# Last expert layer of a two-layer graph block: gated expert rows added into DRAM, instead of gathered and summed in SBUF

## The reference, cut to what matters

```python
def _L1_ffn_ref(x, Wg, bg, W1, b1, W2, b2):          # 8 experts, hidden width 384
    xf = x.reshape(-1, d)                            # x is the layer norm of the tokens
    logits = xf @ Wg.T + bg
    probs = softmax(logits)
    top2_vals, top2_idx = top_k(probs, 2)
    cw = zeros((n, 8)).at[arange(n)[:, None], top2_idx].set(top2_vals)
    h = gelu(einsum('nd,edh->neh', xf, W1) + b1[None])
    y = einsum('neh,ehd->ned', h, W2) + b2[None]
    return einsum('ne,ned->nd', cw, y)
...
x = x + _L1_ffn_ref(_layernorm(x)[None], ...)[0]
```

## Time and profile before

| | |
|---|---|
| Median of three runs | 2000.32 us |
| The profiled execution, its own time | 1999.16 us |
| Its span, first to last instruction | 1997.3 us |
| TensorE (PE) busy | 1838.2 us, 92% |
| VectorE (DVE) busy | 745.1 us, 37% |
| ScalarE (ACT) busy | 401.4 us, 20% |
| GpSimd (POOL) busy | 128.5 us, 6% |
| Mean granted TensorE clock | 0.964 |

### The profile page before, as it was taken

One profiled execution on the slowest core, in us unless ns is written; L12 is line 12 of the kernel. 1 busy time (PEld: TensorE's weight loads), 2 busy tenths in 40 slices (PEclk: granted clock), 3 DMA queues, 4 the chain that ended last, 5 costly groups with the idle time before them and its releaser, 6 DMA issues.

```text
span 1997.3 us, 24539 instructions
## 1 busy us (share of the span) xinstructions
PE 1838.2 (92%) x8418; PEld 1157.3 (58%) x8419; DVE 745.1 (37%) x1688; ACT 401.4 (20%) x1065; POOL 128.5 (6%) x212
## 2 busy tenths in 40 slices
PE   7999999999899999599997999999999999599980
PEld 4555566567533344366666955555588589366550
DVE  3212222597789989411115311151111123311114
ACT  2431210024312212101102421000221211221210
POOL 0000000000000000111114000000000000111105
PEclk9999999999999999699998999999999999699995
DMA  6004000000000101545556111010010011544537
GB/s 185 0 1 150 19 0 1 21 1 1 21 31 31 49 24 42 205 141 189 189 182 180 46 48 48 0 48 0 1 48 1 0 56 47 205 141 174 189 115 235
DMA packets 58060, 153.06 MB, mean 77 GB/s; under 512 B 12526, under 2 KB 23170, under 8 KB 57525
## 3 DMA queue, kind: packets, MB, share of 16 engines
q1 hardware_dynamic: 34053, 87.05, 12.7%
q0 software_dynamic: 13120, 35.86, 6.0%
q10 hardware_dynamic: 10800, 28.98, 4.0%
HBM read 121.37 MB, written 33.99 MB: 78 GB/s over the span
## 4 chain that ended last, share of the span: by engine, by line
PE 81%; DVE 8%; DMA 5%; issue 2%; DVEq 2%; ACT 1%; POOL 1%; ACTq 0%; SPq 0%; POOLq 0%
PE PS L646 23%; PE PS L975 10%; PE PS L656 8%; PE PS L795 5%; PE PS L1016 4%; PE PS L1085 4%; PE PS L717 4%; PE PS L1105 4%; PE PS L1057 4%; DVE WRA L1730 4%; PE PS L1043 3%; PE PS L884 2%; DMA WS<-in_fW 2%; PE PS L893 2%; DVE WRB L1730 2%
## 5 line engine op out<-in xcount | busy, mean ns | idle before, releaser
L646 PE MATMUL PS<-WS,XT 128*125 128x384 f32 x960 | 313.0, 488 | 1.4 <-issue 1.4
L646 PEld LDWEIGHTS PS<-WS,XT 128*125 128x125 f32 x960 | 180.1, 189 | 129.4 <-issue 3.3
L975 PE MATMUL PS<-WS,XGT 128*128 x600 | 199.7, 490 | 0.0
L975 PEld LDWEIGHTS PS<-WS,XGT 128*128 128x128 f32 x600 | 113.2, 192 | 74.6 <-issue 2.2
L656 PE MATMUL PS<-XT,WS 128*128 128x416 f32 (+1 forms) x432 | 151.2, 512 | 0.0
L1730 DVE SCALAR_TENSOR_TENSOR WRA<-RB,U,AT 125x500 f32<-125x500 f32 (+1 forms) x240 | 140.1, 648 | 8.5 <-ACT AT L1205 6.6
L1859 DVE TENSOR_TENSOR YS<-PS,EBB 128x768 f32<-128x768 f32 x48 | 46.0, 958 | 255.3 <-PE PS L975 191.8
L656 PEld LDWEIGHTS PS<-XT,WS 128*128 128x128 f32 x432 | 81.6, 189 | 69.2 <-issue 69.2
L884 PE MATMUL PS<-WRA,F 125*64 125x500 f32 (+1 forms) x480 | 100.1, 535 | 10.1 <-DVE WRA L1730 9.5
L1085 PE MATMUL PS<-WS,XGT 128*128 x288 | 99.6, 497 | 7.7 <-DMA WS<-in_fW 4.9
L1105 PE MATMUL PS<-WS,HT 128*128 x276 | 92.9, 486 | 2.5 <-ACT HT L1417 2.5
(11 more groups left out here) (293 smaller groups left out, 2229.7 us busy)
## 6 DMA issues: line engine op xcount, KB each, us to landing
WS<-in_ewT SPq DMA_DIRECT2D x8, 2304.0 KB, 10.7
expert_rows<-YS ACTq DMA_DIRECT2D x48, 384.0 KB, 2.3
WS<-in_fW SPq DMA_DIRECT2D x16, 1152.0 KB, 7.7
WS<-in_w SPq DMA_DIRECT2D x5, 2304.0 KB, 10.4
xn_rows<-XN ACTq DMA_DIRECT2D x20, 336.0 KB
RB<-expert_rows SPq DMA_DIRECT2D x12, 488.3 KB
WS<-in_wp SPq DMA_DIRECT2D x2, 2304.0 KB, 11.9
WS<-in_W SPq DMA_DIRECT2D x2, 2304.0 KB, 8.1
```

The source lines that it names most:

```text
L646: last = nc.tensor.matmul(ps[0:T, 0:HC], lhsT[:, k, t * T:(t + 1) * T], w[:, k, b * HC:(b + 1) * HC], start=(k == 0), stop=(k == KC - 1))
L975: last = nc.tensor.matmul(PS[:, 4 + 2 * a + b, 0:HC], XGT[:, a, k, :], WS[:, bass.ds(slot, 1), k * C + b * HC:k * C + (b + 1) * HC].rearra ...
```

## The change

In the last layer the expert rows are no longer kept in DRAM by position and gathered by token. SP stores the finished `X` tiles to rows 0 to 1249 of `y_d` during the aggregation. VectorE multiplies each tile of expert rows by the gate of each row, and GpSimd adds the tile's 128 rows to `y_d` at their tokens' rows by an indirect DMA with an adding operation; rows of a tile that stand for no token go to rows from 1250 on. As two tiles can hold the same token, each addition waits until the one before it has landed. At the end SP and ACT copy one half each of rows 0 to 1249 from `y_d` to the result, DRAM to DRAM.

The gate and the row index of each row of each tile come from one more one-hot matmul of 20 steps, the gates cut in three bf16 parts (`TVG`, `GTE`, `SIDX`). The index columns of the gathers and of the additions are now written by VectorE (`row_index`, and `SX` in `expert_rows`), with a semaphore `idx_ready`. The first layer keeps its way of working; its code is only written out.

```diff
 # SP
+        for t in range(NT):
+            sp.wait_ge(dve_emptied, J.emptied("dve", J.at[f"agg2_{t}"] + 1))
+            sp.dma_start(y_d[t * T:t * T + PA, :], X[0:PA, t, :]).then_inc(acc_in, 16)
+            sp.dma_start(y_d[t * T + PA:(t + 1) * T, :], X[PA:T, t, :]).then_inc(acc_in, 16)
         sp.wait_ge(stage_done, 4)
         load(U_FF + 1)
...
-        for t in range(NT):
-            sp.wait_ge(yg_used[3], summed(3, 2 * t + 1))
-            sp.dma_start(out[t * T:t * T + PA, :], X[0:PA, t, :]).then_inc(stored, 16)
-            sp.dma_start(out[t * T + PA:(t + 1) * T, :], X[PA:T, t, :]).then_inc(stored, 16)
-        sp.wait_ge(stored, 32 * NT)
+        sp.wait_ge(y_all, 2)
+        sp.dma_start(out[0:N // 2, :].rearrange("n c -> (n c)").rearrange("(a b) -> a b", b=1920),
+                     y_d[0:N // 2, :].rearrange("n c -> (n c)").rearrange("(a b) -> a b", b=1920)).then_inc(stored, 16)
+        sp.wait_ge(stored, 32)
 # GpSimd
+        def add_rows(n, a, landed):
+            pool.wait_ge(ys_ready, n + 1)
+            for b, count in landed:
+                pool.wait_ge(ys_out[3][b], count * 16)
+            nc.gpsimd.sem_inc(pool_step, 1)
+            nc.gpsimd.indirect_dma_start(out=y_d, out_offset=bass.IndirectOffsetOnAxis(ap=SX[:, a:a + 1], axis=0),
+                                         in_=YS[:, a, :], in_offset=None, compute_op=ALU.add).then_inc(ys_out[3][a], 16)
+        def gather3(k, b):
+            pool.wait_ge(idx_ready, k)
+            nc.gpsimd.sem_inc(pool_step, 1)
+            fetch(3, b)
+        first_gathers(3, 2)
...
+        for m in (2, 3, 4):
+            gather3(m - 1, m % 2)
+        pool.wait_ge(gates_in, 1)
+        pool.wait_ge(acc_in, 32 * NT)
+        add_rows(0, 0, [])
+        with nc.gpsimd.Fori(0, n) as i:
+            gather3(i * 2 + 4, 1)
+            add_rows(i * 2 + 1, 1, [(0, i + 1)])
+            gather3(i * 2 + 5, 0)
+            add_rows(i * 2 + 2, 0, [(1, i + 1)])
+        gather3(n * 2 + 4, 1)
+        add_rows(n * 2 + 1, 1, [(0, n + 1)])
+        gather3(n * 2 + 5, 0)
+        add_rows(n * 2 + 2, 0, [(1, n + 1)])
+        add_rows(n * 2 + 3, 1, [(0, n + 2)])
+        with nc.gpsimd.Fori(0, over) as j:
+            add_rows(n * 2 + j + 4, 0, [(1, n + 2), (0, n + j + 2)])
+            gather3(n * 2 + j + 6, 0)
+        pool.wait_ge(ys_out[3][0], (n + over) * 16 + 32)
+        pool.wait_ge(ys_out[3][1], n * 16 + 32)
+        nc.gpsimd.sem_inc(y_all, 1)
 # TensorE
         hidden(0, 0)
+        pe.wait_ge(gate_parts, 1)
+        for q in range(KT):
+            last = nc.tensor.matmul(PS[:, 7, 0:4 * ETC], OHR[:, q, :], TVG[:, q, :, :].rearrange("p a b -> p (a b)"),
+                                    start=(q == 0), stop=(q == KT - 1))
+        last.then_inc(gates_full, 1)
 # ScalarE: store(3, ...) is gone from the loop; at its end
+        act.wait_ge(y_all, 2)
+        act.dma_start(out[N // 2:N, :]..., y_d[N // 2:N, :]...).then_inc(stored, 16)
 # VectorE, expert_rows
             V.tensor_tensor(YS[:, a, :]..., PS[:, b0:b0 + 2, 0:HC], EBB[L][...], ALU.add).then_inc(y_free[L], 1)
+            if L == 3:
+                V.tensor_copy(SX[:, a:a + 1], SIDX[:, bass.ds(n, 1)])
+                V.drain()
+                V.tensor_scalar(YS[:, a, :], YS[:, a, :], GTE[:, bass.ds(n, 1)], None, ALU.mult).then_inc(ys_ready, 1)
 # VectorE, after route(3, 2, False)
+        V.tensor_copy(GPB[:, 0], GW)
+        V.tensor_tensor(GR, GW, GPB[:, 0], ALU.subtract)
+        V.tensor_copy(GPB[:, 1], GR)
+        V.tensor_tensor(GR, GR, GPB[:, 1], ALU.subtract)
+        V.tensor_copy(GPB[:, 2], GR)
+        for n in range(2):
+            for m in range(3):
+                V.tensor_tensor(tvg[:, :, n, m, :], ot, GPB[:, m, n, :].unsqueeze(2).to_broadcast([T, NT, ETC]), ALU.mult)
+        V.tensor_copy(TVG[:, :, 3, :], OT)
+        V.drain().then_inc(gate_parts, 1)
...
+        def row_index(m, b, turned):
+            dve.wait_ge(turned_n[3], turned)
+            V.tensor_copy(IDX[:, b:b + 1], TOK[:, bass.ds(m, 1)]).then_inc(idx_ready, 1)
         hidden_bias(0, 0)
+        row_index(2, 0, 2)
+        row_index(3, 1, 3)
+        dve.wait_ge(gates_full, 1)
...
+        with nc.vector.Fori(0, pairs) as i:
             for a in range(2):
+                hidden_bias(i * 2 + a + 3, 1 - a)
+                row_index(i * 2 + a + 6, a, i * 2 + a + 6)
+                expert_rows(3, i * 2 + a + 2, a, i + 1)
...
         with nc.vector.Fori(0, over3) as j:
             expert_rows(3, n, 0, turns3 + j)
             hidden_bias(n + 1, 0, turned=n + 2)
-        weighted(3, 0, 0)
-        for t in range(NT):
-            if t + 1 < NT:
-                weighted(3, t + 1, 0)
-            V.drain()
-            weighted(3, t, 1)
+            row_index(n + 2, 0, n + 4)
```

More of the change, by code:

```diff
@@ L584, in fetch, with first_gathers @@
                                          ).then_inc(xg_in[L][b], 16)
-        def gathers(L, k):
+        def first_gathers(L, k):
             for b in range(XNB):
@@ L592, in gathers @@
             pool.wait_ge(tab_ready, k)
[L593 to L613, removed]
@@ L615, in _ @@
-        gathers(1, 1)
-        gathers(3, 2)
+        first_gathers(1, 1)
+        n = nc.gpsimd.value_load(TAB[0:1, 2, 0:1], min_val=1, max_val=ET_MAX // 2 - 1)
+        over = nc.gpsimd.value_load(TAB[0:1, 2, 1:2], min_val=1, max_val=2)
+        with nc.gpsimd.Fori(0, n) as i:
+            for a in range(2):
+                pool.wait_ge(turned_n[1], i * 2 + a + 2)
+                gather(1, i * 2 + a + 2, a)
+        with nc.gpsimd.Fori(0, over) as j:
+            pool.wait_ge(turned_n[1], n * 2 + j + 2)
+            gather(1, n * 2 + j + 1, 0)
@@ new lines, in _ @@
+        pool.wait_ge(xg_in[1][0], (n + over) * 16 + 16)
+        pool.wait_ge(xg_in[1][1], n * 16 + 16)
+        pool.wait_ge(ys_out[1][0], (n + over) * 16 + 16)
+        pool.wait_ge(ys_out[1][1], n * 16 + 16)
+        nc.gpsimd.sem_inc(y_all, 1)
+        for q in range(KT):
+            if q >= YB[1]:
+                pool.wait_ge(yg_used, q - YB[1] + 1)
+            nc.gpsimd.indirect_dma_start(out=YG1[:, q % YB[1], :], out_offset=None, in_=y_d,
+                                         in_offset=bass.IndirectOffsetOnAxis(ap=IDXA[:, q:q + 1], axis=0)
+                                         ).then_inc(yg_in[q % YB[1]], 16)
@@ L618, in _ @@
+        pool.wait_ge(xg_in[3][1], n * 16 + 48)
     @block.tensor
@@ L1327, in _ @@
             columns_of(1, n + 1, 0, used=n + 2)
-            store(1, n, 0)
+            store(n, 0)
         def q1_column(c, q):
@@ L1406, in _ @@
         nc.scalar.drain().then_inc(ht_ready[3], 1)
-        for b in range(2):
-            nc.scalar.drain().then_inc(ys_out[3][b], 16)
         def gelu(n, a):
@@ L1427, in _ @@
                 gelu(n + 1, 1 - a)
-                store(3, n, a)
         with nc.scalar.Fori(0, over3) as j:
@@ L1431, in _ @@
             hidden_columns(n)
-            store(3, n, 0)
             columns_of(3, n + 1, 0, turned=n + 4, used=n + 2)
             gelu(n + 1, 0)
+        act.wait_ge(y_all, 2)
+        act.dma_start(out[N // 2:N, :].rearrange("n c -> (n c)").rearrange("(a b) -> a b", b=1920),
+                      y_d[N // 2:N, :].rearrange("n c -> (n c)").rearrange("(a b) -> a b", b=1920)).then_inc(stored, 16)
     @block.vector
```

100 lines of the change are left out of this document (68 added, 32 removed).

## The result

The changed kernel takes 1982.85 us (median of 10 runs, 1976.12 to 1998.36) against 2000.05 us for the kernel before in the same session (10 runs, 1995.38 to 2002.29). The ratio is 0.9925, 95% interval 0.9909 to 0.9941: 0.75% faster, some 15 us (12 to 18). The profiled execution took 1982.5 us for a span of 1980.7. The forecast was 1981.0. So the total came out, but not every term of it did: the sum hides one term that was too small by some 7 us.

What follows compares the result with a forecast made beforehand. TensorE was taken to bound most of the kernel, but not the 51.5 us tail. New tail to 1971.4, plus 7.7 (start 3.7, clock 1, loads 3) gives span 1979.1; plus 1.9 gives 1981.0 us, range 1971 to 1994.

Steps and rivals of the forecast that it cites:

- The tail carries the gain: After the last tile: the 51.5 us of gathers, multiply-adds and result stores go, replaced by a shorter tail of additions and copies.
- What ends last ahead of the copies: Tail: the unused tile's gather, not the last addition, ends last before the copies; the addition is covered to about 7.2 us.
- Landing of an addition, 6.2 us: Last layer: an addition lands like a gather plus a plain store, 3.9 + 2.3 us; bounds 3.9 to 10.9.
- Rival D: Loop: additions waiting on each other become the bound and the kernel is slower, about 2047 us at 10.9 us landing; chance 0.16.
- The copies, 16.1 us with the end: End of tail: two DRAM-to-DRAM half copies take 14.4 us, plus 1.2 for the unused gather and 0.5 to the end.
- Rival B: End of tail: the closing copy uses 10 DMA engines and takes 7 us more, 1988 us; chance 0.22.
- Start, 3.7 + 1: Start of the last layer: tile 2's gather comes 3.7 us late behind a bias; a clock fall costs 1 us more.
- Gate work, hidden: Start of the last layer: VectorE's gate steps and 20 extra matmuls (2.5 us) fit into existing waits, cost 0.
- Loads against additions, 3 us: Loop: additions lengthen four exposed weight loads by 0.75 us each, 3 us in all; bounds 0 to 8.
- the step on the loop: Loop: from tile 4 on, later gathers have over 7 us of slack; added work per tile stays hidden.
- Rival C: Loop: additions crowd the weight loads, costing 8 to 12 us instead of 3, 1986 to 1990 us; chance 0.10.
- ScalarE's store, worth nothing: Loop: ScalarE loses its row store and wait; this gains nothing, as TensorE never waits for ScalarE there.

Runs made afterwards that it cites:

- experiment 5: version 3 with the last tile's index column early too: 1965.55 us; then token rows and additions straight into the result, no closing copies: 1954.86; also without the unused gather: 1953.75.
- version 3: Changed kernel with the gathers' index columns written ahead of the hidden tiles' biases, at the layer's start and in its loop: 1962.58 us, ratio 0.9824.
- the last direct version: version 3 with token rows and additions straight in the result, no closing copies and no unused gather: 1953.75 us, ratio 0.9772.
- experiment 8: Changed kernel with every tile's addition made twice, the second after the first has landed: 2081.99 us in one run.
- experiment 2: Changed kernel with the index columns of tiles 2 and 3 written ahead of the bias of hidden tile 0: 1980.70 us, ratio 0.9909.
- experiment 6: Changed kernel and kernel before, each with weight loads cut to the first 128 rows per matrix from the third expert on: 1970.37 and 1992.25 us.
- experiment 1: Changed kernel with the adding operation taken out of the row DMAs, so rows overwrite: 1983.79 us, ratio 0.9923.
- experiment 7: version 3 with the adding operation taken out of the row DMAs: 1968.63 us, ratio 0.9844.

## Why the prediction was right, and where it was not

- **The tail carries the gain.** Right: -27.0 us, measured 24.5 us from the end of the last sum, where 51.5 stood and the forecast had 25.6.
- **What ends last ahead of the copies.** Wrong, at no cost. I had the unused gather end last and the addition covered up to a landing of 7.2 us. The last two tiles come only 5.7 us apart, so the last addition first waits for the one before it (4.96 us of GpSimd's wait) and starts 2.6 us after the sum instead of 1.7; its landing then releases the copies (experiment 5).
- **Landing of an addition, 6.2 us.** Near: the last one lands 5.5 us after issue in version 3, 5.3 in the last direct version. Rival D's condition was the right one (a landing near 8 us): six of the 23 additions, those inside loads, take 7.1 to 8.8 us to their last packet, but never two in a row, and the chain step of the others is 6.4 of 8.7 us (experiment 8). The Trainium skill, page "DMA: Bandwidth & Descriptors", section "Rules for kernel authors", says why the wait can't be left out: an accumulating transfer reads its destination and writes later, and another addition in between is lost. No run here tries that.
- **The copies, 16.1 us with the end.** Right: 16.2. Rival B fell: the DMA share is 1.02 over 12 us of them, which is all 16 engines, and the 1.92 MB of each copy went as 32 packets of 60000 B. The Trainium skill, the same page, section "Why a DMA increments its semaphore by 16 and not by 1", goes by the outermost dimension as the instruction carries it. By that rule the 250 pieces of the source text would be 10 engines. The trace shows 16, so if the rule holds, the instruction carried another shape than the source.
- **Start, 3.7 + 1.** Right: 4.5 in the profile, 5.5 less when undone (experiment 2). The clock did fall, at this wait.
- **Gate work, hidden.** Right. Its matmuls take 1.2 us, not 2.5.
- **Loads against additions, 3 us.** This is the step that failed. The loads cost some 10 us (10.5 from the profile, 10.2 by experiment 6), by a mechanism I did not have. I priced additions by the bytes they move. The adding does count: leaving it out gives 5.5 us of the loop back (experiment 1). But a change of place alone gives back all of the loss and more, with the additions kept (experiment 3), and then leaving out the adding saves nothing in the loop (experiment 7). In the step on the loop I had costed the later gather at nothing, since it has "over 7 us of slack". It has, for its own tile. What I left out is whom it meets: with the column behind the bias, the gather goes out just ahead of the load. The clock (4.9 us of the loss) I had counted only at the start. Rival C had the size (8 to 12 us) and half of the cause: an addition does hold the engines longer (its packets take 2.75 us of all 16, a plain row store's 1.0), but that costs only beside a badly placed gather.
- **ScalarE's store, worth nothing.** Wrong, by 1.4 us in my favour. I had written that TensorE never waits for ScalarE in the loop and for nothing but the weights beside its own work; the waits before have 2.5 us for ScalarE's `HT` copy at the last tile.
- **Why the total came out.** Loads +7.2, last tile -1.3, tail -1.1, start -0.2, and the layer began 3.0 us earlier, which I had not forecast: +1.6 on the span, which was forecast at 1979.1 and came to 1980.7. The right total is luck: the 3.0 us look like the executions' own and not the change's.

## What to carry to other kernels

When an instruction that issues a transfer moves in time, slack of the data is half the question; the other half is which transfer it now stands in front of, so lay its new issue time beside those of the large loads. Write the small things that release other engines (an index, a column) ahead of the work that must wait, as far as their own inputs allow: here that took the ratio from 0.9925 to 0.9824, 20 us, where the whole change had brought 15. And a total that comes out right needs its terms checked: only the split at common points showed the loss in the loop, which smaller terms and an early start had mostly covered. The same holds for experiments: plain rows took as long as additions, yet the loop was 5.5 us shorter and the tail 4.0 longer.

## What was not expected of the hardware

- A transfer from GpSimd issued into a load of 2.36 MB starts late: the additions issued 2.9 us into one get their first packet 4.6 to 5.3 us after issue and the last 7.1 to 8.8; alone it is 2.1 to 2.2 and 4.9 to 5.5. A gather issued 0.9 to 1.5 us ahead of the load has its first packet after 1.7 us, as alone.
- GpSimd is busy 1.59 us with the issue of one 128-row addition, 0.99 with that of a gather; without the adding operation (experiment 1) the same row transfer takes 0.99 too:

```profile
L626 POOL DMA_INDIRECT expert_rows<-YS,SX x23 | 36.5, 1588 | 83.0 <-DVE YS L1918 53.6 <-DMA expert_rows<-YS,SX 25.8 <-issue 3.6
L584 POOL DMA_INDIRECT XG<-xn_rows,IDX x21 | 20.7, 986 | 82.9 <-DVE IDX L2064 82.9
```

- Where a transfer of GpSimd lands last, the span ends some 6 us after it (5.9 to 6.6 in six kernels), where a copy of SP and ScalarE lands last, 0.9 us. What fills the 6 us the trace doesn't show.
- Some 0.2 us decide where a small gather stands beside two large copies: issued 0.54 and 0.78 us ahead of them it landed after 5.6 us, issued 0.13, 0.14 and 0.32 us ahead after 15.2.
- In the last layer TensorE's granted clock fell to 0.50, the 1.2 GHz level, behind its waits of 3.8 us (start) and 8.8 us in two (loads) in the changed kernel. With plain rows, where no wait for weights in the loop was over 2.9 us, it stayed at 1.00, the 2.4 GHz level, there. The length of one wait does not tell it all: near 1615 us the clock fell behind a wait of 1.86 us in the kernel before and held behind one of 1.87 in the changed one.
